# Edge stage and first layer of a four-layer graph network as one stage; logs of counts one band late, edge sums copied last

## What is computed

```python
def _L0_gnn_ref(X, W, edge_src, edge_dst, edge_vals):
    Z = jnp.matmul(X, W)
    msg = Z[edge_src] * edge_vals[:, None]
    agg = jax.ops.segment_sum(msg, edge_dst, num_segments=X.shape[0])
    return jax.nn.relu(agg)
# second layer, its condition:
ph = noise_levels * freqs
emb = jnp.concatenate([jnp.sin(ph), jnp.cos(ph)], axis=-1)
cond = jax.nn.silu(emb @ f_w1 + f_b1) @ f_w2 + f_b2
# whole:
x = _layernorm(x + _L0_gnn_ref(x, L0_gnn_W, src, dst, edge_weight), axis=-1)
x = _layernorm(x + _L1_gnn_ref(x, edge_index, node_vec1, ...), axis=-1)
```

## Time and profile before

| | us |
|---|---|
| median of 3 runs | 2396.46 |
| lowest and highest | 2392.19, 2398.84 |
| profiled execution | 2400.95 |
| its span | 2399.2 |
| PE busy | 2106.9 (88%) |
| DVE busy | 1584.8 (66%) |
| ACT busy | 961.6 (40%) |
| POOL busy | 643.8 (27%) |

### The profile page before, as it was taken

The page is one execution under the profiler, slowest core; times in us unless marked ns, Lnnn a source line. Parts: engine busy times, 40 slices in busy tenths (PEclk is TensorE's granted clock), DMA queues, the critical chain, the costliest instruction groups (busy, mean ns, idle before and its releaser), DMA issues. The chain is left out here.

```text
span 2399.2 us, 38632 instructions
## 1 busy us (share of the span) xinstructions
PE 2106.9 (88%) x14446; PEld 1593.5 (66%) x14446; DVE 1584.8 (66%) x3086; ACT 961.6 (40%) x1418; POOL 643.8 (27%) x472
## 2 busy tenths in 40 slices
PE   6888979999899998899999899999898997878783
PEld 5885537788787887787788687788684544333331
DVE  8995344778564778554778554778655046898974
ACT  1112213666333666333666333666330031243442
POOL 0000015200543200544200544200420000476773
PEclk9999989999999999999999999999999997898997
DMA  1012301789511788511788611688946000000001
GB/s 59 34 45 46 104 23 61 130 149 159 118 57 37 136 141 151 128 41 52 117 146 155 138 38 56 114 148 147 201 103 145 16 20 2 0 0 0 1 1 43
DMA packets 488314, 195.74 MB, mean 82 GB/s; under 512 B 441241, under 2 KB 457625, under 8 KB 488133
## 3 DMA queue, kind: packets, MB, share of 16 engines
q1 hardware_dynamic: 488133, 193.31, 39.2%
HBM read 62.94 MB, written 25.45 MB: 37 GB/s over the span
## 5 line engine op out<-in xcount | busy, mean ns | idle before, releaser
L670 PE MATMUL psum<-turned_probability_parts,values_high 125*128 125x125 bf16 x1600 | 283.1, 223 | 55.0 <-DMA turned_probability_parts<-probability_parts 33.8
L859 DVE CUSTOM_DVE_ANT_0 probabilities<-psum,counts 125x1250 f32<-125x1250 f32 x160 | 233.6, 1460 | 125.7 <-PE psum L672 125.2
L1383 ACT ACTIVATE probabilities<-probabilities,row_peaks 125x1250 f32<-125x1250 f32 x160 | 214.5, 1341 | 177.4 <-DVE row_peaks L863 177.3
L672 PE MATMUL psum<-turned_probability_parts,values_low 125*128 125x125 bf16 x1600 | 282.4, 222 | 0.0
L671 PE MATMUL psum<-turned_probability_parts,values_high 125*128 125x125 bf16 x1600 | 282.2, 222 | 0.0
L1575 DVE SCALAR_TENSOR_TENSOR probability_parts<-probabilities,row_masses,probability_parts 125x1250 bf16<-125x1250 f32 x160 | 245.2, 1533 | 11.4 <-ACT probability_parts L1393 9.0
L1902 POOL TENSOR_TENSOR logs_and_shifts<-logs_by_source,target_shifts_spread 125x1250 f32<-125x1250 f32 x80 | 208.0, 2617 | 126.5 <-ACT target_shifts_spread L2035 67.0
L1393 ACT ACTIVATE probability_parts<-probabilities,row_masses 125x1250 bf16<-125x1250 f32 x160 | 214.0, 1338 | 41.8 <-DVE row_masses L871 34.3
L2141 PE MATMUL psum<-probabilities_turned,values_and_ones 125*65 125x512 f32 (+1 forms) x480 | 200.1, 563 | 22.1 <-ACT probabilities_turned L2052 11.8
L670 PEld LDWEIGHTS psum<-turned_probability_parts,values_high 125*128 125x128 bf16 x1600 | 159.6, 100 | 76.5 <-issue 73.5
L453 ACT ACTIVATE norm_std<-norm_moments,norm_eps 125x1 f32<-125x1 f32 x120 | 35.2, 294 | 345.6 <-DVE norm_moments L449 345.6
(11 more groups left out here) (291 smaller groups left out, 5048.4 us busy)
## 6 DMA issues: line engine op xcount, KB each, us to landing
weight_stage<-in_L_gnn_m_w SPq DMA_DIRECT2D x32, 256.0 KB, 2.7
block_inputs_kept<-nodes SPq DMA_DIRECT2D x8, 896.0 KB
counts_kept<-counts_by_target_rows SPq DMA_DIRECT2D x10, 625.0 KB, 3.6
logs_kept<-counts SPq DMA_DIRECT2D x1, 5468.8 KB
nodes<-block_inputs_kept SPq DMA_DIRECT2D x12, 448.0 KB
turned_probability_parts<-probability_parts SPq DMA_TRANSPOSE x320, 3.6
counts_by_target<-counts_kept SPq DMA_DIRECT2D x2, 2187.5 KB
logs_by_source<-logs_kept SPq DMA_DIRECT2D x1, 4375.0 KB
```

Of the source, the lines that this page charges most:

```text
L670: pe.matmul(out, lh, rh, start=first, stop=False, skip_group_check=True)
L672: return pe.matmul(out, ll, rh, start=False, stop=last, skip_group_check=True)
L859: dve.tensor_tensor_reduce(prob[0:TILE, T % 2, :], scores, fx.count_src[0:TILE, i, 0:NODES], scale, MASKED, ALU.add, ALU.max, p[:, 0:1]).t ...
L1383: nc.scalar.activation(prob[0:TILE, T % 2, :], prob[0:TILE, T % 2, :], ACT.Exp, bias=fx.peak[0:TILE, T % 2, 1:2], accum_out=fx.mass[0:TILE ...
```

## The change

`edge_bands` and `first_layer` become one function and one block, `edge_layer`.

- Edge sums are cut by 128 targets (`GROUPS0` = 10 groups of four bands) and by 128 features: `edge_sum(q, c)` is ten matmuls of 128 columns into a quarter of bank 7. One of them is done after each band from band 5 on (`sums_at`, `SUMS_LAG` = 5), the last five after the last band. ScalarE copies the four of a group together, last in its work of the band (`copy_sums`).
- The transposes of the counts are spread: one piece after each of three bands of four, all into bank 6 (`turn_at`, `turn_unit`, `copy_unit`).
- The noise steps of VectorE are spread over bands 1 to 7, the sine is behind band 9, the first noise product is done in three cuts behind bands 11, 15, 19, the second behind 23, 27, 31. The condition goes straight from PSUM to its place, and its low part is made from PSUM too (`condition_low`).
- The logs are made by groups of 128 columns in place of tiles of rows: ScalarE writes log(count + 2^-60) over the counts (`plain_logs`) behind bands 20, 22, to 34, 39 and 42; VectorE makes mask and scale from the log (`log_group`: less than -1 is absent) one band later.
- The ten products with the weight use banks 0 to 5; the first stands between the last sums, the others follow them. Weight, sums and noise tensors have other places in SBUF.

```diff
-        def unit(u):
-            return psum[:, (6 + u % 2) * BANK:(7 + u % 2) * BANK]
+        TURN_BANK, SUM_BANK = psum[:, 6 * BANK:7 * BANK], psum[:, 7 * BANK:8 * BANK]
+        SUMS_LAG = SPAN + 1
+        INNER_AT, COND_AT, SINE_AT = {11: 0, 15: 1, 19: 2}, {23: 0, 27: 1, 31: 2}, 9
+        LOGS_AFTER = {20 + 2 * q: q for q in range(GROUPS0 - 2)}
+        LOGS_AFTER[BANDS - 1] = GROUPS0 - 2
+        def turn_at(b):
+            return (b // SPAN - 1, b % SPAN) if b >= SPAN and b % SPAN < 3 and b // SPAN <= GROUPS0 else None
+        def sums_at(b):
+            g = b - SUMS_LAG
+            return (g // CHUNKS, g % CHUNKS) if 0 <= g < GROUPS0 * CHUNKS else None
+        def width(q):
+            return min(128, NODES - 128 * q)
+        def product_bank(t):
+            return psum[0:TILE, (t % 6) * BANK:(t % 6 + 1) * BANK]
...
+            sp.wait_ge(ready, 1)
+            for c in range(CHUNKS):
+                sp.dma_start(w_sb[c][:, :], w0[c * 128:(c + 1) * 128, :]).then_inc(w_loaded, 16)
...
+            sp.wait_ge(log_ready, GROUPS0)
+            for a, z in ROW_PARTS:
+                sp.dma_start(log_rows.rearrange("(t p) s -> p t s", p=TILE)[a:z], fx.count_src[a:z, :, 0:NODES]).then_inc(fx.logs_kept, 16)
...
+            def noise_step(b):
+                if b == 1:
+                    dve.wait_ge(zeroed, 5)
+                    step(dve.tensor_copy(lane[:, 3:4], lane_i[:, :]))
...
+                if b == 2:
+                    dve.wait_ge(n_loaded, 144)
+                    step(dve.tensor_scalar(phase[:, :], phase[:, :], lane[:, 0:1], None, ALU.mult))
...
+                if b == 7:
+                    step(dve.tensor_scalar(phase[:, :], phase[:, :], lane[:, 2:3], 3.1415925, ALU.add, ALU.min))
+                    dve.tensor_scalar(phase[:, :], phase[:, :], -3.1415925, None, ALU.max).then_inc(emb_ready, 1)
...
+            def condition_low(k):
+                (a, z), rows = CUTS[k], slice(64, 96)
+                dve.wait_ge(cond_ready, k + 1)
+                dve.scalar_tensor_tensor(fx.cond[rows, a:z], TURN_BANK[rows, 0:z - a], fb2[rows, 0:1], fx.cond[rows, a:z].bitcast(F32),
+                                         ALU.add, ALU.subtract).then_inc(cond_low, 1)
+            def log_group(q):
+                counts = count_src[0:TILE, :, 128 * q:128 * (q + 1)]
+                dve.wait_ge(log_plain, q + 1)
+                if q >= 1:
+                    dve.wait_ge(log_ready, q)
+                step(dve.tensor_scalar(absent[0:TILE], counts, -1.0, MASKED, ALU.is_lt, ALU.mult))
+                dve.scalar_tensor_tensor(counts, counts, HDIM1 ** 0.5, absent[0:TILE], ALU.mult, ALU.add).then_inc(log_ready, 1)
...
+                noise_step(b)
+                if b - 1 in COND_AT:
+                    condition_low(COND_AT[b - 1])
+                if b - 1 in LOGS_AFTER:
+                    log_group(LOGS_AFTER[b - 1])
                 begin = end
             weights_of(BANDS - 1)
+            log_group(GROUPS0 - 2)
+            log_group(GROUPS0 - 1)
+            for i in range(TILES + 1):
+                if i < TILES:
+                    here = fx.nodes[0:TILE, i, :]
+                    if i == 0:
+                        dve.wait_ge(sums, GROUPS0 * CHUNKS)
+                    dve.wait_ge(prod, i + 1)
+                    dve.scalar_tensor_tensor(here, product_bank(i), 0.0, here, ALU.max, ALU.add).then_inc(added, 1)
...
-            def turn_group(q):
-                pe.wait_ge(band_copied, SPAN * (q + 1))
-                for u in range(3):
-                    U = 3 * q + u
-                    if U >= 2:
-                        pe.wait_ge(unturn, U - 1)
-                    for j in range(4 * u, min(4 * u + 4, TILES)):
-                        mm = pe.transpose(unit(U)[:, (j % 4) * TILE:(j % 4 + 1) * TILE], count_src[0:TILE, j, q * 128:(q + 1) * 128],
-                                          ident[0:TILE, 0:TILE])
-                    mm.then_inc(turn, 1)
+            def turn_unit(q, u):
+                if u == 0:
+                    pe.wait_ge(band_copied, SPAN * (q + 1))
+                pe.wait_ge(unturn, 3 * q + u)
+                for j in range(4 * u, min(4 * u + 4, TILES)):
+                    mm = pe.transpose(TURN_BANK[:, (j % 4) * TILE:(j % 4 + 1) * TILE], count_src[0:TILE, j, q * 128:(q + 1) * 128],
+                                      ident[0:TILE, 0:TILE])
+                mm.then_inc(turn, 1)
+            def inner_piece(k):
+                a, z = CUTS[k]
+                pe.wait_ge(emb_ready, 2)
+                pe.wait_ge(unturn, 3 * (INNER_BAND[k] // SPAN))
+                pe.matmul(TURN_BANK[0:COND, 0:z - a], fw1[:, :], turns[:, a:z], start=True, stop=True).then_inc(inner_prod, 1)
+            def condition_piece(k):
+                a, z = CUTS[k]
+                pe.wait_ge(inner_ready, 3)
+                pe.wait_ge(unturn, 3 * (COND_BAND[k] // SPAN))
+                pe.matmul(TURN_BANK[0:96, 0:z - a], fw2[:, :], inner[:, a:z], start=True, stop=True).then_inc(cond_prod, 1)
+            def edge_sum(q, c):
+                if c == 0:
+                    pe.wait_ge(summed, min(SPAN * (q + 1), BANDS))
+                    pe.wait_ge(sums_ready, CHUNKS * q)
+                n = width(q)
+                for k in range(TILES):
+                    mm = pe.matmul(SUM_BANK[:, c * 128:c * 128 + n], fx.nodes[0:TILE, k, c * 128:(c + 1) * 128],
+                                   weight_src[0:TILE, k, q * 128:q * 128 + n], start=(k == 0), stop=(k == TILES - 1))
+                mm.then_inc(sums, 1)
+            def first_product(t):
+                pe.wait_ge(sums_ready, CHUNKS * -(-TILE * (t + 1) // 128))
+                if t >= 6:
+                    pe.wait_ge(added, t - 5)
+                for c in range(CHUNKS):
+                    mm = pe.matmul(product_bank(t), sum_t[c][:, t * TILE:(t + 1) * TILE], w_sb[c][:, :], start=(c == 0), stop=(c == CHUNKS - 1))
+                mm.then_inc(prod, 1)
+            def after_band(b):
+                if turn_at(b):
+                    if b - 1 in INNER_AT:
+                        pe.wait_ge(inner_ready, INNER_AT[b - 1] + 1)
+                    if b - 1 in COND_AT:
+                        pe.wait_ge(cond_low, COND_AT[b - 1] + 1)
+                    turn_unit(*turn_at(b))
+                if b in INNER_AT:
+                    inner_piece(INNER_AT[b])
+                if b in COND_AT:
+                    condition_piece(COND_AT[b])
+                if sums_at(b):
+                    edge_sum(*sums_at(b))
+            INNER_BAND, COND_BAND = list(INNER_AT), list(COND_AT)
...
-                if b % SPAN == 0 and b > 0:
-                    turn_group(b // SPAN - 1)
+                if b == SUMS_LAG:
+                    pe.wait_ge(x_loaded, 16)
+                if b == INNER_BAND[0]:
+                    pe.wait_ge(n_loaded, 144)
+                after_band(b)
                 begin = end
-            turn_group(GROUPS0 - 1)
+            for b in range(BANDS, BANDS + SUMS_LAG):
+                after_band(b)
+                if b == BANDS:
+                    pe.wait_ge(w_loaded, 16 * CHUNKS)
+                    pe.wait_ge(band_copied, BANDS)
+                    pe.wait_ge(summed, BANDS)
+                    first_product(0)
+            for t in range(1, TILES):
+                first_product(t)
...
-            def copy_group(q):
-                if q >= 2:
+            def copy_unit(q, u):
+                if u == 0 and q >= 2:
                     act.wait_ge(fx.counts_kept[q % 2], 16 * (q // 2))
-                for u in range(3):
-                    U, n = 3 * q + u, min(4, TILES - 4 * u) * TILE
-                    act.wait_ge(turn, U + 1)
-                    nc.scalar.activation(kept[:, q % 2, 4 * u * TILE:4 * u * TILE + n], unit(U)[:, 0:n], ACT.Copy).then_inc(unturn, 1)
+                n = min(4, TILES - 4 * u) * TILE
+                act.wait_ge(turn, 3 * q + u + 1)
+                nc.scalar.activation(kept[:, q % 2, 4 * u * TILE:4 * u * TILE + n], TURN_BANK[:, 0:n], ACT.Copy).then_inc(unturn, 1)
+            def copy_sums(q):
+                n = width(q)
+                act.wait_ge(sums, CHUNKS * (q + 1))
+                for c in range(CHUNKS):
+                    nc.scalar.activation(sum_t[c][:, q * 128:q * 128 + n], SUM_BANK[:, c * 128:c * 128 + n], ACT.Copy).then_inc(sums_ready, 1)
+            def plain_logs(q):
+                act.wait_ge(turn, 3 * q + 3)
+                if q == 0:
+                    act.wait_ge(zeroed, 4)
+                counts = count_src[0:TILE, :, 128 * q:128 * (q + 1)]
+                nc.scalar.activation(counts, counts, ACT.Ln, bias=fx.tiny[0:TILE, :]).then_inc(log_plain, 1)
+            def after_band(b):
+                if turn_at(b):
+                    copy_unit(*turn_at(b))
+                if b == SINE_AT:
+                    act.wait_ge(emb_ready, 1)
+                    nc.scalar.activation(turns[:, :], phase[:, :], ACT.Sin).then_inc(emb_ready, 1)
```

(28 more changed lines are left out.)

249 lines of the change are left out of this document (80 added, 169 removed).

## The result

| | before | after |
|---|---|---|
| median, us | 2397.25 (20 runs) | 2391.98 (20 runs) |
| lowest and highest | 2392.19, 2414.62 | 2386.89, 2396.32 |
| ratio after / before | | 0.9971, 95% interval 0.9959 to 0.9983 |
| profiled execution and its span | 2400.95, 2399.2 | 2392.28, 2390.4 |
| start of the next stage | 343.61 | 331.12 |

The change makes the kernel 0.29% faster, 5.3 us. The forecast was 2373.0 with a range of 2363 to 2390, so it is wrong: the sign is right, the size is more than four times too large. The next stage was to begin 23.2 us earlier and begins 12.5 earlier; and what comes behind it is not the same either.

What follows compares the result with a forecast made beforehand. VectorE bounds the edge stage, TensorE the first layer; merged, TensorE bounds. Its terms sum to 317.0 us plus 3.4 tail, next stage at 320.4 instead of 343.6, 23.2 less: 2377.8 profiled, median 2373, range 2363 to 2390.

Steps and rivals of the forecast that it cites:

- The start: Before band 5: VectorE bounds, noise steps in bands 1 to 4 add 4.4 us, band 5's products start at 49.1.
- Noise in bands 5 to 7 [...] cost nothing: Edge stage: VectorE's noise steps in these bands and the log groups cost nothing as long as the sums cover them.
- The median of the runs stands 4.5 lower: Whole kernel, last step: from a profiled execution of 2377.8 us after the change to a median of 2373.
- Nothing later depends on the absolute time: Behind the merged stage: only the write of the logs depends on it, 27 us of transfers, ending 9 us before the stage.
- what would make it wrong: Later stages: the prediction calls itself wrong if one after the merged stage changes its length by more than a few us.
- The base: Start of the next stage: 320.4 in place of 343.6, 23.2 us less, taken from the profiled execution of 2400.95 us.
- The sums: Edge sums on TensorE: 800 halves of 128 columns at 0.110 us, 88.0 us; ends 0.108 (-2 us) and 0.135 (+20 us).
- the slower rival: Edge sums: weight load not hidden behind 128 columns, 0.216 us per half, 85 us more, 2458; chance 0.05.
- all seams: About 70 new places where TensorE changes its kind of work: 0 to 6.5 us, taken as 3.
- VectorE beneath the sums: Bands with sums: TensorE needs about 5.8 us per band, VectorE 5.3 in the mean, so VectorE's work is covered.
- The lockstep rival: Edge stage: VectorE's added steps come on the path band by band, 21.6 us in full, 2395; chance 0.10.
- The clock: TensorE in the merged stage: granted clock should be 1.00 from band 5 to the products' end.

Runs made afterwards that it cites:

- the first experiment: Changed kernel with VectorE's wait behind each noise step of bands 1 to 7 moved behind the next band's one-hots; 2385.76 us, ratio to before 0.9952.
- the second: Against the first experiment, all noise steps five bands later, noise products and logs moved back with them; 2377.51 us, ratio to before 0.9918.

## Why the prediction was wrong

**The start, the failed step.** "The noise steps now stand in its bands 1 to 4 [...] together 4.4 us". The durations were right (0.85 and 0.80, against 0.87 and 0.80 in the earlier trace rows). What was left out is the wait behind each step, which the diff shows and the working never names. In the kernel before it cost next to nothing, since behind it came only the next noise step (212.63 to 215.27 for three). In the new place the reading of a band's registers is queued behind it: 1.86 us more per band. The Trainium skill, "Perfetto Trace Analysis", section "Sequencer Loop", has engine instructions go into a queue and control instructions start when they are read; a wait that must be over before the next instruction is read, and a register reading of some length behind it, fit that and the rows of the noise steps. The section also has an engine instruction wait for its semaphores in that queue, by which the reading could go on beside it; the log steps do not bear that out, since there the wait stands at the second step (L367) and the 1.86 us count from its end all the same. How the reading is held up therefore stays open; that it is, the first experiment shows. How much of the 1.86 us is the reading itself is in no row. Band 5 began at 55.17 instead of 49.1, 6.1 us: four gaps are 7.4, less 0.2 for steps that were shorter than the forecast's 4.4, and less 1.1 because VectorE was sooner at band 2 than in the kernel before (the weights in band 1 began at 28.48 and not 29.03, and a wait of 0.57 is gone).

**"Noise in bands 5 to 7 [...] cost nothing".** Wrong, by the same step: bands 5 to 7 take 77.77 - 55.17 = 22.6 us where the forecast has 17.4. The sums of these bands cover a step of 1.4 us but not one of 3.3 with the gap: without the waits they take 17.9 (50.17 to 68.08 in the first experiment). The low clock is not the reason, since with it kept up for longer they take 22.6 again (54.68 to 77.28). So the forecast is 11.3 us off at band 8, and at 331.1 against 320.4 it is 10.7 off: the rest of the sum holds. The first experiment gives 9.7 of it back, the second another 5.3; with the noise left out the stage ends at 314.3, and the forecast's sum without its 4.4 has 316.0.

**The whole miss.** The median is 19.0 us above the forecast. The end of the stage is 10.7 of it and the later part 3.7, by the first traces. The remaining 4 to 5 come from the last step, "The median of the runs stands 4.5 lower": that was the distance in the kernel before, and in the changed kernel the profiled execution and the median are 0.3 apart (2392.28 and 2391.98).

**"Nothing later depends on the absolute time".** The first attention stretch bears it out, and it is beside the point. Its length depends on the program ahead of it, and the later part is 3.7 us longer in each pair of traces. The prediction named this as what would make it wrong, but gave it no price, for the trace of before could give none. The medians (5.3 us gained, where the stage alone gains 10.0 to 12.5) put it at 5 to 7.

**The base.** The gain was taken from one profiled execution whose early part, 343.6, is 3.4 us longer than that of the second trace of the same kernel. About half of that is the granted clock in the first edge sums: 22.77 us at 0.93 in the first trace, 21.15 us at 1.00 for the same work in the second. The forecast's end of the stage, an absolute time, does not suffer from it; the difference to before does. Against 340.2 it would have been 19.8 and not 23.2.

**The sums, right.** More than a quarter of the time of the new stage (88 of 317 us) hung on the price of a half with 128 columns, between 0.108 and 0.135, with 0.216 as the slower rival. All edge sums of the changed kernel (duration ns lowest/median/highest, first and last start), then TensorE in order of time at one of 128 columns:

```profile
L492 PE MATMUL psum<-weights,nodes x800: 253/275/378, 59.8 to 296.5; 125*128 125x128 f32 x144, 125*128 125x98 f32 x16
```

```profile
281.43 2.40 PE L492 MATMUL psum<-weights,nodes 125*128 125x128 f32 x20
283.67 3.60 PE L502 MATMUL psum<-first_weight,edge_sums_turned 128*125 128x512 f32 x8
```

By the starts, a piece of 20 halves and the seam behind it take 83.47 - 81.15 = 2.32 us, 0.116 each with the seam in, and 283.67 - 281.43 = 2.24, 0.112, where another matmul follows at once. The 60 last ones, all of 98 columns, take 296.63 - 289.96 = 6.67, 0.111 each. The forecast had 0.110, and 3.0 us for all seams. The slower rival is refuted. Its rule, in the Trainium skill, "TensorE: Matmul & The Clock Gate", section "The mechanism", that a load goes ahead of running matmuls only on other row groups (or, as the section also says, into a background weight buffer), does not hold in this trace as far as the row groups go: 125 rows are in use in every half and loads are hidden all the same. The same page's section "LDWEIGHTS (loading the stationary operand)" has a load take the number of its columns / 1.2 ns, by which 128 columns are an estimated 107 ns; the trace agrees. A half that streams 98 columns comes every 0.111 us like one that streams 128, though by width it would be 0.083 (98/128 of the 0.108 that the forecast took for the stream). Both load 128 columns. So in the last sums it is not the stream that sets the pace, but the load or something else that goes with each half.

**VectorE beneath the sums, right.** The lockstep rival expected waits of TensorE for one-hots behind the log bands. There are none from 77 to 300 us. In bands 5 to 7, those with noise, 5.2 us came on the path (22.6 against 17.4), but by the waits: with late waits 0.5 are left. The experiment with the logs in the same band shows how near the rival was: without the lag its 21.6 us would have been 46.

**The clock.** Expected was 1.00 from band 5 on; it was 0.86 between 54 and 78 us, and 1.00 from band 8 on. The kernel in which it was kept up shows that in bands 2 to 4 this cost nothing of its own: its band 8 begins at 77.28, against 77.77, and its band 2 was 0.5 us ahead already (33.30 against 33.79).
